# A graph network kernel's prologue: the order of clearing, weight turning and table building

## The reference

```python
h = relu(layernorm(x))
for W_msg, Wih, Whh, bih, bhh in two_layers:
    msg = concat([h[src], edge_attr]) @ W_msg.T
    agg = segment_sum(msg, dst, n_nodes)
    gi, gh = agg @ Wih.T + bih, h @ Whh.T + bhh
    r = sigmoid(gi_r + gh_r); z = sigmoid(gi_z + gh_z)
    h = (1 - z) * tanh(gi_n + r * gh_n) + z * h
return x + h
```

## Time and profile before

| | us |
|---|---|
| median of 3 runs | 3290.52 (3289.2 to 3294.56) |
| the profiled execution | 3279.4 |
| its span, first to last instruction | 3277.7 |
| PE busy in the span | 2630.1 (80%) |
| POOL busy | 2324.6 (71%) |
| DVE busy | 1530.0 (47%) |
| ACT busy | 999.1 (30%) |

### The profile page before, as it was taken

How to read it: one execution, slowest core, us unless ns; L and a number is a source line. 1 busy time by engine, 2 the same in 40 slices (tenths; PEclk the granted TensorE clock), 3 DMA queues, 4 the chain that set the end, 5 groups by cost and what they waited for, 6 DMA issues and landing times.

```text
span 3277.7 us, 74395 instructions
## 1 busy us (share of the span) xinstructions
PE 2630.1 (80%) x20375; PEld 2360.7 (72%) x20376; DVE 1530.0 (47%) x4895; ACT 999.1 (30%) x2343; POOL 2324.6 (71%) x2389
## 2 busy tenths in 40 slices
PE   0689889899898898898975777787787787787887
PEld 0578778788787787787855676687677677686675
DVE  5544455454454544545443444444444445444444
ACT  5212223232232333332341222232232233333333
POOL 4477777777777776776717777777777777777772
PEclk9988798798798898988986777777787787887888
DMA  7233333333333333333315222222222222222221
GB/s 195 56 88 86 86 94 90 85 94 88 87 93 88 85 91 82 92 80 80 88 33 128 54 55 58 56 62 55 61 59 58 60 63 60 64 60 62 65 61 43
DMA packets 350922, 249.44 MB, mean 76 GB/s; under 512 B 226506, under 2 KB 312334, under 8 KB 350628
## 3 DMA queue, kind: packets, MB, share of 16 engines
q0 software_dynamic: 75232, 155.02, 17.5%
q1 hardware_dynamic: 254617, 70.47, 10.3%
q10 hardware_dynamic: 20779, 20.48, 2.1%
HBM read 226.51 MB, written 19.20 MB: 75 GB/s over the span
## 4 chain that ended last, share of the span: by engine, by line
PE 35%; POOL 30%; issue 16%; DVE 6%; DVEq 4%; DMA 3%; ACT 3%; ACTq 1%; SPq 1%; POOLq 1%
POOL rows L666 30%; PE ps_v L762 9%; PE ps_win L802 8%; PE ps_win L786 4%; PE ps_q L755 3%; DVEq L1187 2%; PE ps_c L755 2%; PE ps_b L879 1%; PE ps_b L880 1%; PE ps_d L866 1%; PE ps_d L895 1%; ACT hr L1366 1%; PE ps_a L886 1%; DVEq L1217 1%; PE ps_c L888 1%
## 5 line engine op out<-in xcount | busy, mean ns | idle before, releaser
L666 POOL DMA_INDIRECT rows<-h_table,idx x1156 | 1153.2, 998 | 485.3 <-issue 376.2
L666 POOL DMA_INDIRECT rows<-x_table,idx x1156 | 1144.5, 990 | 410.4 <-issue 402.1
L802 PE MATMUL ps_win<-onehot,rows 128*128 128x80 f32 x4624 | 743.3, 312 | 202.5 <-DMA rows<-x_table,idx 162.8
L802 PEld LDWEIGHTS ps_win<-onehot,rows 128*128 128x128 f32 x4624 | 663.7, 221 | 248.7 <-issue 145.9
L762 PE MATMUL ps_v<-hr,a_blk 125*128 125x128 f32 x4800 | 715.2, 319 | 0.0
L762 PEld LDWEIGHTS ps_v<-hr,a_blk 125*128 125x128 f32 x4800 | 698.4, 235 | 0.8
L1385 ACT COPY a_blk<-ps_q 125x224 f32<-125x224 f32 (+5 forms) x504 | 223.8, 480 | 856.3 <-PE ps_q L755 763.7
L1115 DVE SCALAR_TENSOR_TENSOR v_hot<-v_cur,lane 128x42 bf16<-128x42 f32 (+13 forms) x1180 | 435.1, 425 | 0.0
L786 PE MATMUL ps_win<-onehot,attr 128*64 128x80 f32 x3128 | 312.2, 253 | 120.2 <-DVE onehot L1130 80.4
L755 PE MATMUL ps_q<-v_hot,lo_hot 128*125 128x28 bf16 (+5 forms) x3696 | 289.4, 222 | 139.9 <-DVE v_hot L1115 117.7
L755 PEld LDWEIGHTS ps_q<-v_hot,lo_hot 128*125 128x125 bf16 x3696 | 272.5, 151 | 151.2 <-DVE v_hot L1115 128.9
(11 more groups left out here) (191 smaller groups left out, 2038.3 us busy)
## 6 DMA issues: line engine op xcount, KB each, us to landing
attr<-in_edge_attr_dram SPq DMA_DIRECT2D x390, 128.0 KB
rows<-h_table,idx POOLq DMA_INDIRECT x1156
rows<-x_table,idx POOLq DMA_INDIRECT x1156
dst_in<-in_dst_dram SPq DMA_DIRECT2D x678, 2.0 KB
idx<-in_src_dram SPq DMA_DIRECT2D x576, 2.0 KB
x_table<-out_sb ACTq DMA_DIRECT2D x50, 125.0 KB
attr<-in_x_dram ACTq DMA_DIRECT2D x50, 125.0 KB
out_dram<-out_sb ACTq DMA_DIRECT2D x50, 125.0 KB
```

The source lines that it names most:

```text
L666: nc.gpsimd.indirect_dma_start(out=rows[0:parts, s, j, :], out_offset=None, in_=table[:, :], in_offset=bass.IndirectOffsetOnAxis(ap=idx[0: ...
L802: mm = nc.tensor.matmul(ps_win[r % 2][:, 0:WIN], rows[0:parts, rr, j, :], onehot[0:parts, r % 2, j, :], start=(j == 0), stop=(j == TILES - 1))
```

## The change

Temporaries in `aggT` get new columns, in the order in which they are last read: first `dst_rows`, `stat` and `stat_b` (3,080 columns, up to a new mark `CLEAR_FIRST`), then the parts of src and dst, the raw biases and the raw weights (6,280 columns, up to `CLEAR_EARLY`, now 9,360), then the rest that DVE's tables need (2,806 columns, up to `CLEAR_LATE` = 12,166). The biases are turned and added before DVE's first reduction, the weights are turned right after the src and dst parts, and the clearing is shared among ACT (two parts), DVE and POOL.

```diff
+        CLEAR_FIRST = room[0]          # after dst_rows, stat, stat_b
...
+        b_raw = start_only(12, P)      # both moved up, behind t_dst ... tm
+        w_raw = start_only(P, 2 * 8 * P).rearrange("p (l k m) -> p l k m", l=2, k=8)
+        CLEAR_EARLY = room[0]
+        max_all = start_only(P, NSTAT) # and gidx, touch, ..., bend: moved down to here
...
-        b_raw = start_only(12, P)
-        CLEAR_EARLY = room[0]
-        w_raw = start_only(P, 2 * 8 * P).rearrange("p (l k m) -> p l k m", l=2, k=8)
+        CLEAR_LATE = room[0]
 POOL, after the loads of the weights:
+            nc.gpsimd.memset(aggT[:, CLEAR_LATE:COLS], 0.0)
             nc.gpsimd.memset(edgeT[0:D, :], 0.0).then_inc(edge_zeroed, 1)
 PE:
             pe.wait_ge(consts_made, 1)
+            pe.wait_ge(w_loaded, 16 * 12)
+            nc.tensor.transpose(ps_a[:, 0:12], b_raw[:, :], ident[0:12, 0:12]).then_inc(b_turned, 1)
             pe.wait_ge(stat_ready, 1)
...
             pe.wait_ge(tiles_ready, 1)
+            pe.wait_ge(bias_ready, 1)
...
             mm.then_inc(tiles_turned, 1)
-            pe.wait_ge(need_ready, 1)
-            nc.tensor.matmul(ps_q[0:1, 0:STEPS], ones[...], bend[...], ...).then_inc(ready_ps_ready, 1)
-            pe.wait_ge(w_loaded, 16 * 12)
-            pe.wait_ge(tables_ready, 1)
-            nc.tensor.transpose(ps_a[:, 0:12], b_raw[:, :], ident[0:12, 0:12]).then_inc(b_turned, 1)
+            pe.wait_ge(base_kept, 1)
             for layer in range(2):
                 for k in range(8):
...
             pe.wait_ge(w_kept, 16)
-            pe.wait_ge(bias_ready, 1)
+            pe.wait_ge(need_ready, 1)
+            nc.tensor.matmul(ps_q[0:1, 0:STEPS], ones[...], bend[...], ...).then_inc(ready_ps_ready, 1)
 DVE, after the normalisation:
+            dve.wait_ge(b_turned, 1)
+            chained(nc.vector.tensor_copy(bT[:, :], ps_a[:, 0:12]))
+            for layer in range(2): ...          # the two b_gate sums
+            ins.then_inc(bias_ready, 1)
...
-            chained(nc.vector.tensor_copy(max_all[:, :], ps_win[1][:, 0:NSTAT]))
+            nc.vector.tensor_copy(max_all[:, :], ps_win[1][:, 0:NSTAT]).then_inc(base_kept, 1)
+            dve.wait_ge(base_kept, 1)
...
-            dve.wait_ge(b_turned, 1)            # with the copy and the two sums, up to bias_ready
-            dve.wait_ge(w_turned, 16)
-            nc.vector.memset(aggT[:, CLEAR_EARLY:COLS], 0.0).then_inc(sums_zeroed, 1)
+            dve.wait_ge(tables_ready, 1)
+            nc.vector.memset(aggT[:, CLEAR_EARLY:CLEAR_LATE], 0.0).then_inc(sums_zeroed, 1)
 ACT, after the normalisation:
+            act.wait_ge(base_ps_ready, 1)
+            nc.scalar.copy(aggT[:, 0:CLEAR_FIRST], zero[...])
             for i in range(16):                 # the copies of the turned weights
...
-            act.wait_ge(tables_ready, 1)
+            act.wait_ge(tiles_turned, 1)
             act.wait_ge(bias_ready, 1)
-            nc.scalar.copy(aggT[:, 0:CLEAR_EARLY], zero[...]).then_inc(agg_zeroed, 1)
+            nc.scalar.copy(aggT[:, CLEAR_FIRST:CLEAR_EARLY], zero[...]).then_inc(agg_zeroed, 1)
```

More of the change, by code:

```diff
@@ L169, in build @@
         stat_b = start_only(SROWS, 2 * SCOLS * P).rearrange("p (w k m) -> p w k m", w=2, k=SCOLS)
[L170 to L179, removed]
+        CLEAR_FIRST = room[0]
         NE = TCOLS * P
@@ L195, in build @@
         tb_b = a_blk[0:TROWS, 0:4, :]
+        b_raw = start_only(12, P)
+        w_raw = start_only(P, 2 * 8 * P).rearrange("p (l k m) -> p l k m", l=2, k=8)
+        CLEAR_EARLY = room[0]
+        max_all = start_only(P, NSTAT)
+        gidx = start_only(P, NSTAT)
+        touch = start_only(P, NSTAT)
+        span_i = start_only(1, NSTAT, I32)
+        cend = start_only(P, 1)
+        eps = start_only(P, 1)
+        ones = start_only(P, 1)
+        late = start_only(P, 1)
+        need = start_only(P, 1)
+        bend = start_only(P, STEPS)
         row_of = start_only(VC, BT)
@@ L271, in build @@
         w_kept = sem("w_kept")
+        base_kept = sem("base_kept")
         b_turned = sem("b_turned")
@@ L725, in _ @@
             mm.then_inc(tiles_turned, 1)
-            pe.wait_ge(need_ready, 1)
-            nc.tensor.matmul(ps_q[0:1, 0:STEPS], ones[0:CHUNKS, :], bend[0:CHUNKS, :],
-                             start=True, stop=True).then_inc(ready_ps_ready, 1)
-            pe.wait_ge(w_loaded, 16 * 12)
-            pe.wait_ge(tables_ready, 1)
-            nc.tensor.transpose(ps_a[:, 0:12], b_raw[:, :], ident[0:12, 0:12]).then_inc(b_turned, 1)
+            pe.wait_ge(base_kept, 1)
             for layer in range(2):
@@ L740, in _ @@
             pe.wait_ge(w_kept, 16)
-            pe.wait_ge(bias_ready, 1)
+            pe.wait_ge(need_ready, 1)
+            nc.tensor.matmul(ps_q[0:1, 0:STEPS], ones[0:CHUNKS, :], bend[0:CHUNKS, :],
+                             start=True, stop=True).then_inc(ready_ps_ready, 1)
             pe.wait_ge(ln_relu, LN_STEPS)
@@ L965, in _ @@
                                                    op0=ALU.mult, op1=ALU.mult).then_inc(ln_shift, 1)
+            dve.wait_ge(b_turned, 1)
+            chained(nc.vector.tensor_copy(bT[:, :], ps_a[:, 0:12]))
+            for layer in range(2):
+                o = 6 * layer
+                ins = nc.vector.tensor_tensor(b_gate[:, layer, :], bT[:, o:o + 2], bT[:, o + 3:o + 5], ALU.add)
+            ins.then_inc(bias_ready, 1)
             dve.wait_ge(dst_rows_loaded, 16 * (2 + SROWS - (FULL - (SCOLS - 1) * SROWS)))
@@ L1063, in _ @@
             nc.vector.tensor_copy(ready_i[0:1, 1:STEPS + 1], ps_q[0:1, 0:STEPS]).then_inc(tables_ready, 1)
-            dve.wait_ge(b_turned, 1)
[L1067 to L1071, removed]
-            dve.wait_ge(w_turned, 16)
-            nc.vector.memset(aggT[:, CLEAR_EARLY:COLS], 0.0).then_inc(sums_zeroed, 1)
+            dve.wait_ge(tables_ready, 1)
+            nc.vector.memset(aggT[:, CLEAR_EARLY:CLEAR_LATE], 0.0).then_inc(sums_zeroed, 1)
             dve.wait_ge(sums_zeroed, 1)
@@ L1368, in _ @@
                     ins.then_inc(ln_relu, 1)
+            act.wait_ge(base_ps_ready, 1)
+            nc.scalar.copy(aggT[:, 0:CLEAR_FIRST], zero[:, 0:1].to_broadcast([P, CLEAR_FIRST]))
             for i in range(16):
@@ L1374, in _ @@
                 nc.scalar.copy(wT[0:part, layer, k, :], ps_win[i % 2][0:part, 0:P]).then_inc(w_kept, 1)
-            act.wait_ge(tables_ready, 1)
+            act.wait_ge(tiles_turned, 1)
             act.wait_ge(bias_ready, 1)
-            nc.scalar.copy(aggT[:, 0:CLEAR_EARLY], zero[:, 0:1].to_broadcast([P, CLEAR_EARLY])).then_inc(agg_zeroed, 1)
+            nc.scalar.copy(aggT[:, CLEAR_FIRST:CLEAR_EARLY],
+                           zero[:, 0:1].to_broadcast([P, CLEAR_EARLY - CLEAR_FIRST])).then_inc(agg_zeroed, 1)
             again_count = act.alloc_register("act_again_count")
```

## The result

The changed kernel takes 3275.8 us (median of 15 runs) where the kernel before took 3288.83 in the same series: a ratio of 0.996, 95% interval 0.9949 to 0.9971, which is 13.2 us less (9.5 to 16.8); the medians differ by 13.0. The forecast was 12.8 us less and 3277.7 us.

A forecast was written before the change was run, and what follows sets the result against it. POOL's gather stream, set by its second start, bounds the kernel; from tables' end to first head group 15.98 us becomes 0.40 + 0.03 + 2.40 + 0.32 = 3.15, 12.8 us off the 3290.52 median: 3277.7 us, range 3267 to 3289.

The forecast's parts named there:

- The bound: POOL's gathers: time is when their stream starts, plus a stream of nearly fixed length, plus the last chunks.
- second start: POOL's gathers going on after the first eight, once PE summed the first head group: about 105.0 instead of 117.79 us.
- The prediction's own sign of being wrong: Core wrong if gathers restart at 105 us with under 8 us gained, or later because ACT's second clear outlasts DVE's.
- Weights beside the tables: PE's 16 weight turns, right after the turned parts, take 6.71 us and end about 91.9 us, under DVE's tables.
- ACT's clears: Two parts, 2.63 us ending at 77.5 and 5.36 us ending at 97.3, off the path with 4.3 us to spare.
- Biases: On DVE before the reduction at 65.24 us; they move the reduction, turning and tables 0.40 us later.
- POOL's clear: 462 extra columns on POOL, 0.4 us, costing nothing because POOL then idles 44 us up to 73.04.
- DVE's clear: 2,806 columns directly behind the tables, now on the path: 2.40 us, from 99.22 to 101.62.
- DVE's table stretch: DVE's 12.37 us from 85 to 98 with ACT and PE beside it: 0 taken, at worst 0.9 us longer.
- PE's start: First 16 head products take 2.37 us; about 3.6 us idle ahead; a possible 0.4 us further gain not counted.
- The rivals: Turning not beside tables (0.05, gain 3.2 us); layer 0's end gives gain partly back (0.10) or makes it slower (0.05).
- the end of layer 0: 1300 to 1640 us, PE's clock falling from 0.90: each 0.01 costs 3.4 us; partly back 0.10, slower 0.05.

The follow-up runs named there:

- turns late: Changed kernel with the 16 weight turns put back behind the tables; ratio 0.9999 to the kernel before.
- six and twelve clears: Changed kernel with DVE's last clear done six or twelve more times; ratios 1.0035 and 1.0069 to the kernel before.
- freed gathers: Changed kernel without POOL's head-group wait in layer 0's first pass, ratio 0.9943 to before; second kernel also moves five tables to ACT's clear, 0.9935.
- one clear: Changed kernel without ACT's first clear, ACT clearing columns 0 to 9,360 in one piece after the weight copies; ratio 0.9963 to the kernel before.
- tables to ACT: Changed kernel with five 392-column tables moved to ACT's part, DVE clearing 846 columns instead of 2,806; ratio 0.9948 to the kernel before.

## Why the prediction was right

*The bound.* POOL's stream sets the time, and its second start sets the stream: starts moved by -12.1, -3.0, +6.1 and +24.9 us against before (changed kernel, turns late, six and twelve clears) gave -13.2 and -15.1, -0.3, +11.5 and +22.7 us. All but the six-clear one hold the start's move in their interval, and that one misses it by 1.1 us. This holds while PE keeps up: with the freed gathers the ninth gather comes 34.6 us earlier than before (83.19 against 117.79), and 18.7 us are gained, because PE then holds POOL.

The length of the stream is fixed only to some 10 us. From the second start to layer 0's last gather, the eight kernels that keep POOL's wait for the head take between 1,544.3 us (the earliest start, 103.51) and 1,554.6 (start 123.85), and the latest start, 142.68, takes 1,546.2; no order by start shows. Layer 1's gathers take 1,497.4 to 1,500.3 us. The prediction's rows also left out 1640 to 1724 us, where POOL stands 13.36 us for indices and 56.34 us ahead of layer 1's first gather; after the change these are 13.36 and 56.16, so the sum didn't suffer.

The prediction's own sign of being wrong, gathers restarting at 105 us and an end less than 8 us earlier, came true in the two profiles (3.2 us), and the 3266.6 us forecast for the profiled execution was 3276.25. The runs, 13.2 and 15.1 us less, say otherwise; the profiled execution before was an uncommonly short one. That the forecast of the median, 3277.7, lies 1.9 us from the measured one is partly luck, with intervals of 7 us.

*Weights beside the tables.* Forecast from 85.2 to 91.9 us, measured 85.01 to 91.76; DVE's tables took 0.09 us longer beside them. *ACT's clears.* 2.63 and 5.36 us forecast, 2.76 and 5.43 measured, the second with 5.3 us to spare where 4.3 were forecast. *Biases.* They take 0.35 us ahead of the reduction (64.93 to 65.28), forecast 0.40. That their old place would have cost as much was not tried. *POOL's clear.* 0.50 us, hidden.

*DVE's clear: the term that was mis-sized.* I took 0.03 us of gap and 2.40 us. The clear itself was 2.40 as forecast, but the profile shows DVE idle for 0.65 us ahead of it, 0.62 more than forecast. The row of the kernel before hid the same: its clear starts at 106.21 us though the last turn ends at 99.11 + 6.51 = 105.62, and I had put that gap down to waiting. With gap, 2,806 columns cost 3.05 us and 846 cost 1.00: 1.05 ns a column. After the last clear the gap is 0.28 us, so it lies ahead of a clear and grows with it: the recorded length leaves out about the first fifth. The Trainium skill, "VectorE: DVE Perf Modes", section "Zero memsets can be issued as uint32 (trn2)", says that a memset takes one cycle per element. With the clock of 0.96 GHz in the page's section "Specifications" that makes an estimate of 2.92 us for 2,806 columns; the trace comes near it only if the gap is counted, with 3.05 us against 2.40.

*DVE's table stretch.* From the reduction to the tables' last copy it took 33.35 us before (65.24 to 98.59) and 33.83 after (65.28 to 99.11). I had allowed up to 0.9 us for neighbours in the later part, from 85 us on; that part grew by 0.09 (84.90 to 98.59 before, 85.33 to 99.11 after). The other 0.39 us came earlier, between 73 and 79 us, beside POOL's first gathers. The two traces side by side, DVE and POOL before:

```profile
73.34 0.43 DVE L982 TENSOR_SCALAR aggT<-aggT 102x512 f32<-102x512 f32 x1
73.68 0.40 DVE L983 TENSOR_SCALAR aggT<-aggT 102x4 f32<-102x4 f32 x1
...
75.86 0.42 DVE L988 COPY a_blk<-aggT 102x512 f32<-102x512 f32 x1
...
77.11 0.43 DVE L991 TENSOR_SCALAR aggT<-aggT 102x512 f32<-102x512 f32 x1
```

```profile
74.39 1.26 POOL L666 DMA_INDIRECT rows<-h_table,idx  x1 [0.30 <-issue]
75.95 1.25 POOL L666 DMA_INDIRECT rows<-h_table,idx  x1 [0.30 <-issue]
```

and after:

```profile
73.37 0.65 DVE L992 TENSOR_SCALAR aggT<-aggT 102x512 f32<-102x512 f32 x1
73.94 0.15 DVE L993 TENSOR_SCALAR aggT<-aggT 102x4 f32<-102x4 f32 x1
...
75.92 0.62 DVE L998 COPY a_blk<-aggT 102x512 f32<-102x512 f32 x1
...
77.36 0.57 DVE L1001 TENSOR_SCALAR aggT<-aggT 102x512 f32<-102x512 f32 x1
```

```profile
74.07 0.97 POOL L670 DMA_INDIRECT rows<-h_table,idx  x1 [0.30 <-issue]
75.35 0.94 POOL L670 DMA_INDIRECT rows<-h_table,idx  x1 [0.30 <-issue]
```

The first long instruction costs nothing, since the small one behind it is shorter by as much and the next starts at 74.12 us in both. The copy at 75.92 and the one at 77.36 cost 0.2 and 0.14 us. Where they are short, the second and third gathers are long, and the other way round.

All ten traces fall into these two cases. In seven (the changed kernel twice, turns late, one clear, six and twelve clears, tables to ACT) the first gather starts 7.44 or 7.45 us after DVE's reduction, DVE has the long instructions, and the second and third gathers take 0.94 to 0.97 us. In the other three (before, and both kernels with freed gathers) it starts 7.59 to 7.80 us after, DVE's are short, and these gathers take 1.24 to 1.26. Two of the three have the changed prologue, so these 0.4 us are not its price: they go with when the first gather falls against DVE's work, and they are part of the 1.05 us by which the head was earlier with freed gathers.

The Trainium skill, "SBUF — State Buffer", section "Who interferes with whom", has DVE's copies and tensor_scalars in a two-port mode share a port pair with GpSimd under an exclusive lock that goes to whoever issues first. These rows agree in that one of the two engines pays, up to 0.2 us an instruction on DVE's side and 0.3 on POOL's. They don't show the order: the first gather is recorded as starting before DVE's tensor_scalar in both, 0.30 us (73.04 to 73.34) and 0.65 us (72.72 to 73.37) ahead. The run without ACT's first clear excludes ACT; the lock itself is argued from the pattern.

*PE's start.* The first 16 products take 2.36 us after 4.46 us of idle (some 3.6 forecast), as they took 2.37 after 10.05, so the 0.4 us that I left out were rightly left out.

*The rivals.* The turning did lie beside the tables. For the end of layer 0, the price that the rival named wasn't paid: from 1300 to 1640 us the granted clock is 0.90 in both profiles. The 2.8 us that this pair lost between the second start and layer 0's last gather (1,548.0 to 1,550.8 us) are within the scatter above. The move of the first head group closes by terms: 12.83 forecast, less 0.62 for the clear's gap and 0.48 for DVE's table stretch, more 0.05 for the biases and 0.05 for the shorter gap behind the clear, is 11.83 us. From the start of the last row of the normalisation to the first head group it is 49.61 us before (65.16 to 114.77) and 37.79 after (64.85 to 102.64), 11.82 less. That row came 0.31 us earlier in the second execution, which makes the 12.13.

## What to carry to other kernels

Find the stream that hardly ever waits, and ask what starts it: a prologue step on that path is worth its length, however small its share of the span, as long as the stream's next partner, here PE, keeps up. Clearing, turning and loading that the path's engine doesn't need itself can lie beside it, if data that die early are put where they can be cleared early; which columns a temporary gets decides who may clear them and when. Once ACT was off the path, splitting its clear earned nothing; look at what is last then, here DVE's own clear and the gathers' wait for the head.

## What was not expected of the hardware

A DVE clear is recorded 0.65 us (2,806 columns) or 0.24 us (846) after DVE's instruction ahead of it had ended, though the two have the same instruction ahead and the same wait: for this instruction the idle time ahead belongs to its cost.

PE's first products are slow at a granted clock of 1.00, the higher of its two levels (2.4 GHz), which stood at 1.00 in the stretch ahead of them, too, where PE did next to nothing (106 to 115 us before, 92 to 102 after). The head before and after, with the clock as the third number from the end:

```profile
115.00:117.00 2.00, 1.33 (x10) 1.36 (x11) 1.13 (x4) 0.00 (x0) 0.00 (x0) 1.00 0.00 0
```

```profile
103.50:105.50 2.00, 1.96 (x15) 1.99 (x16) 0.94 (x5) 0.00 (x0) 0.00 (x0) 1.00 0.00 0
```

Eight products take 1.18 us in the first two head groups against 0.74 us later, in both kernels. Why they are slow no run here shows.
